# A four-stage attention and mixture-of-experts kernel: rounded first-expert weights made in the first attention's tail, second-expert biases loaded in the second's

## The chip, the cores and the metric

The kernel runs on one core of one Trainium2 chip. The metric is the device time of one execution in microseconds (us). Engines are named as in the profile: PE is the matmul engine (PEld its weight loads), DVE the vector engine, ACT the scalar engine, POOL the GpSimd engine and SP the sync engine, which here only issues DMA transfers. A name with q (SPq, ACTq) is that engine's instruction queue, where its DMA issues, drains and waits appear.

## What is computed

Two layers, each a gated cross-attention followed by a gated mixture of experts, all in float32. `x` is 32 batches of 100 tokens by 256, `ctx_768` is 32 batches of 361 rows by 192.

```python
x = x + tanh(g_xattn[0]) * L0_xattn(layernorm(x), ctx_768, Wq, Wk, Wv, Wo, bo)      # 8 heads of 64
x = x + tanh(g_ffn[0])   * L0_ffn(layernorm(x), router, w13, w2)                    # 8 experts, top 2, F = 512
x = x + tanh(g_xattn[1]) * L1_xattn(ctx_768, layernorm(x), mask, ...)               # 4 heads, keys of ctx and of x
x = x + tanh(g_ffn[1])   * L1_ffn(layernorm(x), Wg, W1, b1, W2, b2, W3, b3)         # 16 experts, top 4, F = 256

# L1_ffn, for each expert e, with a routing weight we per token:
h = silu(x2 @ W1[e].T + b1[e]) * (x2 @ W3[e].T + b3[e])
y = y + (h @ W2[e].T + b2[e]) * we[:, None]
```

## The kernel before

The program is a row of blocks, one after the other: a setup (L200), the first attention (`attention0`, L335), the first experts (`experts(…, 0)`, L1504), the second attention (`attention1`, L893) and the second experts (`experts1`, L1812). At the end of a block every engine runs a short drain of its own queue, and none starts the next block until the last engine has drained. In each block every engine has a program of its own, written out by hand as a list of steps; `at(i + k, step)` runs a step for batch `i + k` if there is such a batch, so that several batches are in flight, and semaphores hold the engines together. No planner decides the order: it is the order of the code, engine by engine.

`attention0` takes one batch of 100 tokens at a time. To keep float32 accuracy with faster matmuls, context and key/value weights are split in a rounded part (`c_hi`, `wk_hi`, `wv_hi`) and a rest (`c_lo`, `wk_lo`, `wv_lo`). SP loads `x` and `cT` (four transfers per batch, both double-buffered), stores the new `x` rows and the normalised rows, and, between the loads of batches 1 and 2, issues `fill` (L164 to L170: 16 issues of zeros or start values, for the tables, row buffers and outputs in memory that the later stages scatter into) and `load_attention1` (L180 to L190, the second attention's weights and scales). The load of `x` of batch b+2 waits for POOL's `xb` of batch b (L773), that of `cT` for the reads of `cT` of batch b. The routing steps at the end of each batch (L661 to L705 on DVE) choose two experts per token; POOL scatters table rows (L795) with the token's slot.

`experts(…, 0)` processes 57 tiles of 128 slots, sorted by expert. It starts with a *plan*: seventeen small DVE operations in a chain (L1555 to L1571) that turn the tokens per expert in `base` into each tile's expert, row and start, three PE transposes and three DVE casts (L1573 to L1575). SP's `slots` loads and POOL's gathers (L1512) wait for the plan. Its up-projection weights are split as well: ACT writes `w_hi` (rounded copy, 8 operations of 128x2048, L1679) and the rest is formed in place, `w13 - w_hi`: for experts 0 and 1 on POOL (L1531), for 2 to 7 on DVE after the plan (L1580). PE waits for all eight before its first tile. `w_hi` has a buffer of its own in this block.

`attention1` has a similar pipeline for the second layer. It begins on DVE with 16 memsets of `base`, a memset of the 25 padding rows of the whole `kv` buffer (L1323), of `ctx` padding, mask and a few others; the last one counts up `ready`, for which SP's first load, PE, ACT, POOL and DVE itself wait. In each round SP issues `x1in` of batch i+4, then `ctx` and mask of batch i+3. At its end the plan for the second experts is made here too, and SP and ACT write the end markers of each expert's rows (`empty_tails`, L890 and L891); SP ends its block after waiting for all of them.

`experts1` processes 115 tiles. SP loads rows (`xr`, L1885), ACT first issues three bias loads (L1906: `b1`, `b3`, `b2`, each broadcast to 128 partitions, 2048 KB) and then runs its tile work, DVE waits for all three and then adds `bias` to the up-projection `psG` into `pre` (L1843). `psG` holds two tiles, so PE can do tiles 0 and 1 before DVE has read `psG`.

## Time and profile before

| | us |
|---|---|
| median of 3 runs | 2112.01 (2111.58 to 2114.26) |
| the profiled execution | 2113.48 |
| its span in the trace | 2111.7 |
| engine busy in the span | PE 1932.3 (92%), DVE 1338.0, POOL 1147.6, ACT 930.0 |
| first attention, up to the release of its block | to 733.4 |
| first experts | 733.4 to 1071.2 |
| second attention | 1071.2 to 1727.5 |
| second experts | 1727.5 to the end |

The profiled execution is 1.47 us above the median and its span 1.78 us shorter than its time. In a row of the timeline the first number is the start in us from the span's start, the second how long the piece took, then come engine, line, operation, output and inputs with shapes, the number of instructions taken together (x16), and in brackets the idle time of the engine before it with what ended it. Where several instructions are taken together in one row, the duration is from the first's start to the last's end.

### The profile page before, as it was taken

How to read it: one execution, taken by the hardware profiler on the slowest of the kernel's cores; microseconds unless marked ns; L12 is line 12 of the kernel's file. 1: busy time of each engine (PE TensorE's matmuls, PEld its weight loads, DVE VectorE, ACT ScalarE, POOL GpSimd, SP SyncE). 2: the span in 40 equal slices, each digit the busy share in tenths (PEclk: the TensorE clock that was granted, in tenths of full speed). 3: DMA queues.
4: the chain of work that ended last, by engine and by line, in shares of the span. 5: the costliest groups of instructions: out<-in, count | busy, mean ns of one | idle time of the engine just before them, and what ended most of it. 6: DMA issues, size and time to landing. Idle time of an engine off the chain costs nothing. (4 is left out here: it accounts for less than half of the span.)

```text
span 2111.7 us, 39938 instructions
## 1 busy us (share of the span) xinstructions
PE 1932.3 (92%) x11418; PEld 1348.0 (64%) x11418; DVE 1338.0 (63%) x4050; ACT 930.0 (44%) x2321; POOL 1147.6 (54%) x1375
## 2 busy tenths in 40 slices
PE   5999999999999459999939999999999839999997
PEld 4777777777777348888825555555555525666664
DVE  3677777777777453222336888888888734566564
ACT  2444444434343233233216767666667503333332
POOL 1344444444444345445526888888888723454554
PEclk8999999999999679999979999999999758999999
DMA  6011111111107013333311111111112754555555
GB/s 170 27 31 37 32 35 36 31 39 28 40 27 260 9 26 53 54 52 51 52 32 34 51 51 52 56 56 53 54 54 69 253 167 98 89 92 88 94 89 75
DMA packets 140294, 142.24 MB, mean 67 GB/s; under 512 B 31626, under 2 KB 130674, under 8 KB 139832
## 3 DMA queue, kind: packets, MB, share of 16 engines
q1 hardware_dynamic: 94282, 86.60, 13.9%
q0 software_dynamic: 37888, 44.51, 13.3%
q10 hardware_dynamic: 7918, 8.57, 1.3%
q8 instruction: 105, 1.72, 0.4%
q14 instruction: 101, 0.83, 0.1%
HBM read 89.88 MB, written 51.94 MB: 67 GB/s over the span
## 5 line engine op out<-in xcount | busy, mean ns | idle before, releaser
L779 POOL TENSOR_SCALAR prob<-prob,rc 100x363 f32<-100x363 f32 x256 | 157.0, 623 | 354.6 <-DVE rc L634 354.6
L1826 POOL DMA_INDIRECT out<-y,xr x115 | 178.0, 1548 | 210.2 <-DVE y L1859 138.1
L1932 PE MATMUL psG<-expert_w,xgT 128*128 x460 | 222.0, 606 | 3.0 <-ACT xgT L1893 3.0
L980 PE MATMUL psJ<-wkv,cTn 96*121 96x512 f32 x384 | 177.7, 600 | 0.0
L1843 DVE TENSOR_TENSOR pre<-psG,bias 128x512 f32<-128x512 f32 x115 | 79.5, 691 | 144.6 <-PE psG L1932 104.1
L558 ACT ACTIVATE prob<-psS,nm 100x361 f32<-100x361 f32 x256 | 141.5, 561 | 53.8 <-DVE nm L629 47.6
L1525 POOL DMA_INDIRECT acc<-y,slots x57 | 90.3, 1584 | 136.5 <-DVE y L1619 131.6
L629 DVE TENSOR_REDUCE nm<-psS 100x2 f32<-100x722 f32 x128 | 115.0, 898 | 70.8 <-PE psS L457 70.6
L1432 POOL DMA_INDIRECT rows<-row,pos_of x128 | 137.1, 1071 | 35.6 <-issue 30.1
L1596 DVE TENSOR_TENSOR hid<-psU,gate 128x512 f32<-128x512 f32 x57 | 39.4, 691 | 159.3 <-PE psU L1716 159.3
L1893 ACT ACTIVATE xgT<-psX 128x256 f32<-128x256 f32 x115 | 44.0, 383 | 212.6 <-PE psX L1923 131.9
L1411 POOL TENSOR_TENSOR rk<-rk,neghalf 121x12 f32<-121x12 f32 x64 | 126.8, 1982 | 5.3
L638 DVE COPY pT<-psT 121x600 f32<-121x600 f32 x128 | 99.1, 774 | 44.9 <-PE psT L465 44.7
L563 ACT ACTIVATE oT<-psO 128x100 f32<-128x100 f32 x128 | 32.3, 253 | 210.1 <-PE psO L478 206.7
L1949 PE MATMUL psD<-expert_w,hT 128*128 x460 | 119.7, 383 | 1.2 <-ACT hT L1903 1.2
L1107 ACT ACTIVATE kv<-psJ 121x512 f32<-121x512 f32 (+2 forms) x160 | 88.0, 550 | 69.6 <-PE psJ L980 68.9
L1932 PEld LDWEIGHTS psG<-expert_w,xgT 128*128 128x128 f32 x460 | 79.9, 194 | 60.5 <-issue 60.5
L465 PEld LDWEIGHTS psT<-ident,prob 100*121 100x121 f32 x768 | 95.0, 187 | 27.8 <-POOL prob L779 20.4
L544 ACT ACTIVATE kT<-psJ 128x361 f32<-128x361 f32 x128 | 60.9, 476 | 116.4 <-PE psJ L420 116.4
L457 PE MATMUL psS<-kT,qT 64*100 64x361 f32 x512 | 110.9, 507 | 0.7 <-ACT prob L558 0.7
L465 PE MATMUL psT<-ident,prob 100*121 100x100 f32 x768 | 108.8, 278 | 2.4 <-POOL prob L779 2.4
L1754 PE MATMUL psD<-expert_w,hT 128*128 x456 | 108.0, 380 | 1.6 <-ACT hT L1674 1.6
(307 smaller groups left out, 5110.1 us busy)
## 6 DMA issues: line engine op xcount, KB each, us to landing
xr<-rows SPq DMA_DIRECT2D x115, 136.5 KB
expert_w<-in_L_ffn_moe_w SPq DMA_DIRECT2D x8, 1024.0 KB
bias<-in_L_ffn_b ACTq DMA_DIRECT2D x3, 2048.0 KB, 15.9
ctx<-in_ctx SPq DMA_DIRECT2D x32, 181.5 KB
cT<-in_ctxT SPq DMA_DIRECT2D x32, 180.5 KB
cT<-in_ctxT SPq DMA_DIRECT2D x64, 90.2 KB
expert_w<-in_L_ffn_moe_w SPq DMA_DIRECT2D x8, 512.0 KB
expert_w<-in_L_ffn_W1T SPq DMA_DIRECT2D x16, 256.0 KB
```

What stands on the lines that cost most here:

```text
L457: t.matmul(psS[0:N, h, 0:S], qT[rows, b % 2, p, :], kT[rows, b % 2, p, :], start=True, stop=True).then_inc(s_mm, 1)
L465: mm = t.transpose(psT[0:CH, h, j * N:(j + 1) * N], prob[:, (2 * p + h) % 4, j * CH:(j + 1) * CH], ident[0:N, 0:N])
L558: s.activation(prob[:, q, 0:S], psS[0:N, h, 0:S], ACT.Exp, bias=nm[:, q:q + 1], accum_out=rs[:, q:q + 1]).then_inc(exp_done, 1)
L629: v.tensor_reduce(nm[:, q2:q2 + 2], psS[0:N, :, 0:S], AX, ALU.max, negate=True).then_inc(max_done, 1)
L779: g.tensor_scalar(prob[:, q, :], prob[:, q, :], rc[:, q:q + 1], 1.0, ALU.mult, ALU.mult).then_inc(prob_done, 1)
L980: mm = t.matmul(ph[0:rows, 0:cols], lhs, wt[:, k, :], start=k == 0, stop=k == 1)
L1411: g.tensor_tensor(rk[:, b % 3, lo:hi, :], rk[:, b % 3, lo:hi, :], neghalf[0:CH, 0:1].unsqueeze(2).to_broadcast([CH, hi - lo, H1]), ALU.pow ...
L1432: g.indirect_dma_start(rows, bass.IndirectOffsetOnAxis(pos[:, b % 4, k:k + 1], 0), row[:, b % 4, :], None).then_inc(slots_out[b % 2], 16)
L1754: mm = t.matmul(psD[:, r, 0:D], hT[:, r, k, :], w2[:, bass.ds(e, 1), k, :], start=k == 0, stop=k == KF - 1)
L1826: g.indirect_dma_start(acc, bass.IndirectOffsetOnAxis(row_token[:, j % RING, :], 0), y[:, j % 4, :], None, compute_op=ALU.add).then_inc(sc ...
L1932: mm = t.matmul(psG[:, r, :], xT[:, r, k, :], w13[:, bass.ds(e, 1), k, :], start=k == 0, stop=k == 1)
L1949: mm = t.matmul(psD[:, r, 0:D], hT[:, r, k, :], w2[:, bass.ds(e, 1), k, :], start=k == 0, stop=k == KF - 1)
```

## The change

Line numbers of code after the change are those of the changed file. The change does six things.

1. **Buffers.** `w_hi` (now `c["w13_hi"]`) gets fixed space that lies over a slab of 64 KB per partition; `attention0`'s big buffers (`wk`, `wv`, `cT`, `c_hi`, `c_lo`, `kT`, `vv`, `qT`, `prob`) are views of the same space. In the second attention `ctx`, `sq`, `kv` and `prob` are views of a second slab, `late`, and the experts' biases (`b2`, then `b1` and `b3`) are other views of it.
2. **Weights.** The eight ACT copies and the rests of experts 0 to 2 move to the last rounds of `attention0`: copies 0 and 1 after the last `oT`, copy 2 after the last `xmT`, copies 3 to 7 at the end; rest 0 on DVE after the last normalisation, rests 1 and 2 at the end of DVE's program. Rests 3 to 7 stay with the experts, on DVE. POOL makes none.
3. **Plan.** The first experts' plan moves to the end of `attention0`, ahead of rests 1 and 2, with its transposes in `psY`.
4. **Start of `attention0` on SP.** `x` and `cT` of batch 2 are loaded before `fill`; `load_attention1` is issued in round 2, after the context load of batch 5.
5. **Start and rounds of `attention1`.** The `kv` memset covers only the first two of the five column blocks of each buffer (25x3072 for 25x7680; which of the three buffers a batch uses is shifted by one) and moves to POOL, which counts up `padded`; ACT and POOL wait for that. `ready` is counted up by the `ctx` memset, and only SP and DVE wait for it, SP after the first `x1in`. Context loads are issued before the `x1in` load of the same round, the other memsets follow.
6. **Biases.** SP issues them as five transfers in the last rounds of `attention1`: `b2` after the store of batch 29, `b1` and `b3` of experts 0 to 5 after that of batch 30, the rest when PE has done the last `oT`. ACT's three issues in `experts1` go.

```diff
@@ attention0, SP
-                for b in range(2):
+                for b in range(3):
                     load_x(b)
                     if b == 0:
                         s.wait_ge(ready, 1)
                     load_c(b)
                 fill(s, dram, c)
-                load_attention1(nc, s, a, c)
-                load_x(2)
-                load_c(2)
...
                     if b + 3 < B:
                         load_c(b + 3)
+                    if b == 2:
+                        load_attention1(nc, s, a, c)
@@ attention0, ACT
+                    if i == B:
+                        s.wait_ge(c["experts0_loaded"], 16 * W0_LOADS)
+                        s.wait_ge(k_mm, 4 * B)
+                        s.wait_ge(v_mm, 3 * B)
+                        make_high(s, c, range(0, 2))
...
+                    if i == B:
+                        make_high(s, c, range(2, 3))
...
+                s.wait_ge(s_mm, H0 * B)
+                s.wait_ge(o_mm, pairs * B)
+                make_high(s, c, range(3, E0))
@@ attention0, DVE
                     at(i - 1, y_norm)
+                    if i == B:
+                        make_low(v, c, range(0, 1))
...
+                steps = Count(plan)
...
+                v.tensor_copy(c["tile_r"][:, :], psY[0:1, P:2 * P])
+                make_low(v, c, range(1, 3))
@@ attention1, SP
-                s.wait_ge(ready, 1)
                 for i in range(-4, B + 1):
+                    if i == -3:
+                        s.wait_ge(ready, 1)
+                    at(i + 3, load_c)
                     at(i + 4, load_x)
-                    at(i + 3, load_c)
+                    if i == B - 1:
+                        s.wait_ge(ct_mm, 2 * B)
+                        s.wait_ge(ssB, B)
+                        s.wait_ge(o_mm, pairs * (B - 2))
+                        s.dma_start(b2, a["L1_ffn_b2"].partition_broadcast(P)).then_inc(c["bias_in"], 16)
+                    if i == B:
+                        s.wait_ge(o_mm, pairs * B)
+                        load_bias(s, 6, E1)
                     at(i - 1, store)
+                    if i == B - 1:
+                        s.wait_ge(o_mm, pairs * (B - 1))
+                        load_bias(s, 0, 6)
@@ attention1, DVE
-                for e in range(E1):
-                    v.memset(c["base"][:, e:e + 1], float(e * REGION))
-                v.memset(kv[96:CH, :, :, :], 0.0)
-                v.memset(ctx[96:CH, :, NCH - 1, :], 0.0)
+                v.memset(ctx[96:CH, :, NCH - 1, :], 0.0).then_inc(ready, 1)
...
+                for e in range(E1):
+                    v.memset(c["base"][:, e:e + 1], float(e * REGION))
@@ attention1, POOL
-                g.wait_ge(ready, 1)
+                g.memset(kv[96:CH, :, 0:2, :], 0.0).then_inc(padded, 1)
+                g.wait_ge(padded, 1)
@@ experts, POOL
-                if L0:
-                    for e in range(2):
-                        g.wait_ge(w_high, e + 1)
-                        g.tensor_tensor(w13[:, e].bitcast(F32R), w13[:, e], w_hi[:, e].bitcast(F32), ALU.subtract).then_inc(w_low, 1)
-                g.wait_ge(plan, PLANNED + 1)
@@ experts, DVE (after the plan, which is gone from here)
                 if L0:
-                    for e in range(2, E):
...
+                    make_low(v, c, range(3, E))
@@ experts1
-                for k in range(3):
-                    s.dma_start(bias[:, :, k, :], a[("L1_ffn_b1", "L1_ffn_b3", "L1_ffn_b2")[k]].partition_broadcast(P)).then_inc(bias_in, 16)
...
-                v.wait_ge(bias_in, 16 * 3)
+                v.wait_ge(c["bias_in"], 16 * BIAS_LOADS)
```

In the order listings a row is one instruction or several alike (x2): line, operation, output, inputs and the output's shape. On SP at the start of the first attention, from the load of batch 1 on, before and after (`cT_117` is `cT`; `table`, `xn`, `acc`, `out` and `rows` are filled from a buffer of zeros, `expert_w`):

```order
L354 DMA cT<-in_ctxT 64x361
L164 DMA table<-expert_w 128x512
L164 DMA table<-expert_w 6x512
L167 DMA xn<-expert_w 128x256
...
L189 DMA wr<-in_L_ffn_WgT 128x2x16
L190 DMA bo<-in_L_xattn_bo 100x256
L345 DMA x<-in_x 100x256
L352 DMA cT<-in_ctxT 128x361
```

```order
L396 DMA cT_117<-in_ctxT 64x361
L387 DMA x<-in_x 100x256
L394 DMA cT_117<-in_ctxT 128x361
L395 DMA cT_117<-in_ctxT 64x361
L396 DMA cT_117<-in_ctxT 64x361
L175 DMA table<-expert_w 128x512
```

The loads of batch 2 moved ahead of all 16 fill issues, and the weight loads of the second attention are no longer between.

On DVE at the end of the first attention (the branch is the end of the block's program, the next one the start of the experts'), from the last steps of the plan on, before and after:

```order
L1570 TENSOR_REDUCE tilet<-tilefirst 128x1
L1571 SCALAR_TENSOR_TENSOR tilet<-tilet,landed 128x1
L1573 CAST tile_s<-psX 1x128
L1574 CAST tile_e<-psX 1x128
L1575 CAST tile_r<-psX 1x128
L1580 TENSOR_TENSOR expert_w<-expert_w,w_hi 128x2048 x6
L1586 TENSOR_TENSOR xg_lo<-psX,xg_hi 128x256
```

```order
L839 SCALAR_TENSOR_TENSOR tilet<-tilet,landed 128x1
L841 CAST tile_s<-psY 1x128
L842 CAST tile_e<-psY 1x128
L843 CAST tile_r<-psY 1x128
L317 TENSOR_TENSOR expert_w<-expert_w,w_hi 128x2048 x2
L377 UNCONDITIONAL_BRANCH
L1640 UNCONDITIONAL_BRANCH
L317 TENSOR_TENSOR expert_w<-expert_w,w_hi 128x2048 x5
L1649 TENSOR_TENSOR xg_lo<-psX,xg_hi 128x256
```

The plan and two of the rests now stand before the block's end, and the experts' block starts on DVE with five rests where it had the plan and six.

On SP at the end of the second attention, after the change (before, four `out` stores stand there in a row, and then the same `base_i` row):

```order
L1014 DMA out<-x 100x256 x2
L1025 DMA late<-in_L_ffn_b 128x4096
L1014 DMA out<-x 100x256
L979 DMA late<-in_L_ffn_b 128x6x256
L980 DMA late<-in_L_ffn_b 128x6x256
L979 DMA late<-in_L_ffn_b 128x10x256
L980 DMA late<-in_L_ffn_b 128x10x256
L1014 DMA out<-x 100x256
L984 TENSOR_LOAD base_i
```

Five bias transfers stand between and around the last stores, ahead of SP's part of `empty_tails`.

## Rows read from the trace of the kernel before

**Rows 1.** The page, part 2: the span in 40 slices of 52.8 us, PE's lines.

```profile
PE   5999999999999459999939999999999839999997
...
PEclk8999999999999679999979999999999758999999
```

**Rows 2.** Windows: length, busy of PE to POOL, granted clock, DMA share, GB/s.

```profile
40.00:50.00 10.00, 8.44 (x40) 7.00 (x42) 4.46 (x9) 2.48 (x7) 2.52 (x5) 0.50 0.01 2
...
50.00:60.00 10.00, 10.00 (x59) 7.25 (x56) 4.14 (x9) 3.26 (x11) 1.39 (x4) 0.82 0.18 47
```

**Rows 3.** Timeline, start of the first attention: POOL, SP queue, ACT, PE.

```profile
23.81 0.72 POOL L773 TENSOR_TENSOR xb<-x,bo 100x256 f32<-100x256 f32 x1
...
34.49 1.30 SPq L354 DMA_DIRECT2D cT<-in_ctxT  x1
...
40.09 0.81 ACT L550 ACTIVATE c_hi<-cT 128x728 fp32r<-128x728 f32 x1 [6.03 <-DMA cT<-in_ctxT]
...
41.27 3.71 PE L430 MATMUL psJ<-xT,wq 128*128 128x100 f32 x16 [5.49 <-ACT xT L540]
```

**Rows 4.** Timeline, end of the first attention and start of the first experts.

```profile
719.24 0.17 DVE L661 COPY sc<-psY 100x8 f32<-100x8 f32 x1 [1.95 <-PE psY L499]
...
723.18 0.21 DVE L687 TENSOR_SCALAR slot<-slot,tmp 100x1 f32<-100x1 f32 x1
...
733.47 14.51 ACT L1679 ACTIVATE w_hi<-expert_w 128x2048 fp32r<-128x2048 f32 x8 [12.53 <-PEq L335]
...
735.61 4.39 DVE L1565 TENSOR_TENSOR tilet<-tile,tilet 128x1 f32<-128x1 f32 x1
...
740.22 4.25 DVE L1567 SCALAR_TENSOR_TENSOR tilet<-tilet 128x1 f32<-128x1 f32 x1
...
747.56 13.30 DVE L1580 TENSOR_TENSOR expert_w<-expert_w,w_hi 128x2048 fp32r<-128x2048 f32 x6
...
751.12 1.81 POOL L1512 DMA_INDIRECT xg<-xn,slots  x1 [6.67 <-DMA slots<-table]
...
761.11 0.66 PE L1708 MATMUL psX<-ident,xg 128*128 128x128 f32 x2 [14.37 <-DVE expert_w L1580]
```

**Rows 5.** POOL's drain at the end of the first attention: duration ns, start us.

```profile
L335 POOLq DRAIN  x1: 5297/5297/5297, 727.9 to 727.9; - x1
```

**Rows 6.** Timeline, start of the second attention.

```profile
1073.75 6.46 DVE L1323 MEMSET kv<- 25x7680 f32 x1 [1.93 <-issue]
...
1083.22 0.43 DVE L1198 BATCH_NORM_STATS2 st<-x1in 100x6 f32<-100x256 f32 x1 [2.15 <-DMA x1in<-acc]
...
1084.27 0.32 SPq L914 DMA_DIRECT2D m<-in_mask  x1
...
1087.35 0.88 DVE L1182 BATCH_NORM_STATS2 cst<-ctx 121x6 f32<-121x192 f32 x3 [3.49 <-DMA m<-in_mask]
```

**Rows 7.** Timeline, end of the second attention and start of the second experts.

```profile
1702.09 0.29 SPq L920 DMA_DIRECT2D out<-x  x1
...
1713.70 11.19 SPq L891 DMA_DIRECT2D rows<-rows  x8
...
1727.62 9.54 ACTq L1906 DMA_DIRECT2D bias<-in_L_ffn_b  x3
...
1728.68 10.30 SPq L1885 DMA_DIRECT2D xr<-rows  x8
...
1737.74 3.78 PE L1932 MATMUL psG<-expert_w,xgT 128*128 x4 [2.47 <-ACT xgT L1893]
...
1749.51 0.69 DVE L1843 TENSOR_TENSOR pre<-psG,bias 128x512 f32<-128x512 f32 x1 [30.48 <-DMA bias<-in_L_ffn_b]
...
1757.28 1.88 PE L1932 MATMUL psG<-expert_w,xgT 128*128 x4
```

**Rows 8.** Timeline, one round in the middle of the second attention.

```profile
1429.59 0.31 SPq L914 DMA_DIRECT2D m<-in_mask  x1
...
1434.38 0.42 DVE L1198 BATCH_NORM_STATS2 st<-x1in 100x6 f32<-100x256 f32 x1
```

More of the change, by code:

```diff
@@ L281, in router_tiles, with bias_views, make_high, make_low @@
     )
+def bias_views(c):
+    b2 = c["late"][:, 0:E1 * F1].rearrange("p (e f) -> p e f", e=E1)
+    b13 = c["late"][:, E1 * F1:3 * E1 * F1].rearrange("p (e k f) -> p e k f", e=E1, k=2)
+    return b2, b13
+BIAS_LOADS = 5
+def make_high(s, c, which):
+    w13, w2 = expert_views(c, 0)
+    w_hi = c["w13_hi"]
+    for e in which:
+        s.activation(w_hi[:, e], w13[:, e], ACT.Copy).then_inc(c["w13_high"], 1)
+def make_low(v, c, which):
+    w13, w2 = expert_views(c, 0)
+    w_hi = c["w13_hi"]
+    for e in which:
+        v.wait_ge(c["w13_high"], e + 1)
+        v.tensor_tensor(w13[:, e].bitcast(F32R), w13[:, e], w_hi[:, e].bitcast(F32), ALU.subtract).then_inc(c["w13_low"], 1)
 def attention0(nc, maker, a, dram, c):
@@ L534, in _ @@
                     at(i, values, 2)
+                t.wait_ge(plan, PLANNED - 1)
+                t.matmul(psY[0:1, 2 * P:3 * P], tf[:, 5:6], ident[:, :], start=True, stop=True)
+                t.matmul(psY[0:1, 0:P], tf[:, 2:3], ident[:, :], start=True, stop=True)
+                t.matmul(psY[0:1, P:2 * P], tf[:, 3:4], ident[:, :], start=True, stop=True).then_inc(plan, 1)
             @block.scalar
@@ L1057, in y_logits @@
                     mm.then_inc(lg_mm, 1)
-                t.wait_ge(ready, 1)
                 for i in range(-3, B + 2):
@@ L1635, in _ @@
             def _(s):
-                s.wait_ge(plan, PLANNED + 1)
                 def load(j):
@@ L1676, in _ @@
                 if L0:
-                    s.wait_ge(w_loaded, w_total)
-                    for e in range(E):
-                        s.activation(w_hi[:, e], w13[:, e], ACT.Copy).then_inc(w_high, 1)
+                    pass
                 else:
@@ L1800, in experts1 @@
         xT = sb("xgT1", [P, 2, 2, P])
-        bias, pre = sb("bias1", [P, E, 3, F]), sb("pre1", [P, 2, 2 * F])
+        pre = sb("pre1", [P, 2, 2 * F])
+        b2, b13 = bias_views(c)
         gate, hid, hT = sb("gate1", [P, 2, F]), sb("hid1", [P, 2, F]), sb("hT1", [P, 2, KF, P])
```

159 lines of the change are left out of this document (83 added, 76 removed).

## The prediction

> **What bounds the kernel now.** I read the page's busy slices first. PE is at nine tenths or more in both attentions and the second experts and nearly that in the first experts; it dips at four places: the first slice and the three changes of block [rows 1]. The granted clock dips at the same places: PE comes back from idle time at a lower clock. So inside the stages only less PE work would help, and this change removes none; what it can win lies in the four dips. The windows and the timeline say what each waits for.
>
> Start of the first attention: SP issues the context of batch 2 only at about 34.5, behind the fill and the second attention's weights; ACT waits 6.03 us for it and PE then has an idle 5.49 [rows 3]. After it PE runs at 0.50 of its clock in 40 to 50 and at 0.82 in 50 to 60 [rows 2]. Start of the first experts: the block is released at 733.4 because POOL's drain ends last [rows 5]; DVE then works through the plan until 747.56, two of its steps taking 4.39 and 4.25 us, then through six rests, 13.30 us, and PE begins at 761.11, released by DVE [rows 4]. Start of the second attention: DVE is free only at 1083.22 - 2.15 = 1081.07, after a 6.46 us memset, and SP's first load waits for that; context statistics begin at 1087.35 [rows 6]. Start of the second experts: ACT's queue is held 9.54 us by bias issues, DVE waits 30.48 us for the biases until 1749.51, and PE starts the up-projection of its fourth tile at 1757.28 [rows 7].
>
> **A, order on SP at the start.** In the new order x of batch 2 waits for POOL's `xb` of batch 0, which ends at 23.81 + 0.72 = 24.5, and its context is issued right behind, at about 25 to 26, against 34.5. ACT wanted it at 40.09 - 6.03 = 34.06 [rows 3], so it has 8 us to arrive. The wait of 5.49 goes. The lower clock behind it goes too: from 41.27 to 60 PE did 8.73 x 0.50 + 10 x 0.82 = 12.6 us of work at full clock in 18.7 us [rows 2], 6.2 lost. I take off 1 us for short waits that were hidden behind the long one. A = 5.49 + 6.2 - 1.0 = 10.7; bounds 5.5 (the wait only) and 11.7. The fill now starts some 3 us later and the weight loads two rounds later: nobody needs the latter before 1071, and SP's issues in round 2 hold up loads that are a whole round early.
>
> **B, end of the first attention and start of the first experts.** One ACT copy is 14.51 / 8 = 1.81 us, one rest on DVE 13.30 / 6 = 2.22 [rows 4]. Rest 0 goes in after the last normalisation, where DVE was idle for 1.95 until 719.24: from 717.29 to 719.51, so what follows is 0.27 late, and DVE's attention work ends at 723.18 + 0.21 + 0.27 = 723.66. The plan took from 733.5 to 747.56, 14.1 us; two steps stalled for 4.39 and 4.25 where a step of that size takes 0.21, as at 723.18 [rows 4]. I put the stalls down to POOL's two rests, which run then and now go. So the plan takes 14.1 - 8.2 = 5.9: until 729.5, where DVE had been idle. Rests 1 and 2 follow until 734.0. ACT is no limit: even if its eight copies began only at 723.2, copy 2 would be there at 728.6 and copy 7 at 737.7. POOL's drain would end at 727.9 + 5.3 + 0.3 = 733.5 [rows 5], DVE at 734.0 with a short drain behind it, so the release moves from 733.4 to about 734.4. Then five rests, 11.1 us, to 745.5, and PE starts 0.25 later, as it did before, at 745.8. B = 761.11 - 745.8 = 15.3. What is late next is the gather of tokens: it needs SP's slots, which are loaded at once now. Before, the first gather came at 751.12, 3.6 us after the plan's end, and took 1.81 with DVE in its rests [rows 4]; the same from 734.4 has it at 738, well ahead. Bounds: 15.5, and 11.7 where the rests on DVE hold POOL's drain (below).
>
> On that the rows show: two small DVE steps grow to 4.39 and 4.25 us while POOL runs tensor operations of its own [rows 4], so the two engines do exclude each other, in that direction. The Trainium skill, "SBUF — State Buffer", section "SBUF: two separate sides", calls this an exclusive lock on a port pair shared by DVE and GpSimd, and adds that a transfer issued by GpSimd cannot write its descriptors while a DVE operation holds it. By that rule the rests would hold what POOL does in its tail and the gathers; the gather of 1.81 us under the rests shows that they don't stop it for long here.
>
> **D, start of the second attention.** The first context load now waits only for the release at 1071.2 and one short memset: `ready` at about 1071.8. The mask's issue, the last of the context's three, follows some 0.8 later (before, it came 3.2 after `ready`, behind two `x1in` loads as well; one issue takes 0.3 [rows 6, 8]), at 1072.6, and the statistics 1087.35 - 1084.27 = 3.08 behind that: 1075.7. D = 1087.35 - 1075.7 = 11.65. The `kv` memset is on POOL: 0.4 of the elements, 2.6 us at DVE's rate, while ACT and POOL first have work to do about 3 us after `ready`; at a third of DVE's rate it would take 7.8 us and cost some 2.5. `base` is needed only by the first routing, several rounds on. D between 9 and 12.
>
> **C, biases.** Six megabytes took from 1727.62 to 1749.51: 6.29 MB in 21.9 us, 287 GB/s [rows 7]. The last 2.5 MB are issued after PE's last `oT`, before the last store, which SP issued at 1702.09; 8.7 us of transfer, so landed by about 1711, ahead of the end markers at 1713.70. DVE's wait goes, and ACT's 9.54 us. Next in line is `xr` of tile 0: issued at 1728.68, there 2.15 later, if it takes what `x1in` took [rows 6], at 1730.8; transpose 0.66 [rows 4] and ACT copy, 1.3 in all, as PE's tile begins: 1732.1 instead of 1737.74. Up-projection of tile 0 at half clock 3.78, of tile 1 the same with 1 us between, to 1740.8; tile 2 to start at 1741. Tile 3 comes 3.0 later at full clock, or 5.6 if the clock is still low, as it was before from 1751.65 to 1757.28. From PE's start at 41.27 the clock was low until about 53.6 (0.82 as the mean of 50 to 60 [rows 2] is 3.6 us at half and the rest at full), 12 us; the same from 1731 is 1743, in the middle of this. I take 1744.5. C = 1757.28 - 1744.5 = 12.8; bounds 9 and 14.
>
> **In the rounds of the second attention** `x1in` is issued behind the context and mask instead of ahead. The mask goes out at 1429.59, so `x1in` at about 1430.0; DVE reads it at 1434.38 [rows 8]. 4.4 us stand against a landing of 2.15, so it costs nothing; it is the one edit that repeats, 29 times. The views over slabs change no instruction.
>
> **Sum.** 10.7 + 15.3 + 11.65 + 12.8 = 50.4. The profiled execution took 2113.48, so 2063.1; it lay 1.47 above the median, which leaves 2061.6, rounded to 2062.
>
> **Rivals.**
> 1. *The rests on DVE hold POOL's drain.* For it: the stalls above, and that rests 1 and 2 lie wholly beside the drain. Against it: the drain took 5.3 us before while DVE stood idle [rows 4, 5], so it waits for something else. Price up to 4.4 us: release at 738, PE at 749.4, B = 11.7, time 2065. Chance 0.14.
> 2. *Only the wait of A goes.* Other short gaps in the first rounds keep the clock low as long as before. For it: even in 40 to 50 PE was busy for only 8.44 of 10 us [rows 2]. Against: the clock rose after that in spite of it. A = 5.5, time 2067. Chance 0.10.
> 3. *The biases delay the tail of the second attention.* Up to 4 MB in the last 25 us run beside POOL's row scatters, which the block's end waits for. The Trainium skill, "DMA: Bandwidth & Descriptors", section "Issuing engines are not separate DMA queues", says that all transfers share 16 engines and interleave, whoever issues them; no row here shows the two together. If the last of them hangs over 1713.70, C falls to 4 to 9, time 2066 to 2070. Chance 0.07.
> 4. *`x1in` comes late.* Behind a batch's context it lands after 1434.4, and each of 29 rounds grows. At 5 us after its issue the loss is 0.6 a round, 17 us, time 2079: 0.03. *Slower than before* is the same mechanism from 6.1 us on: 50.4 / 29 = 1.7 us a round eats all that is won, at 7 us the time is 2137. Against it: nothing in the profile lands so late with the queues this empty. Chance 0.03.
> 5. *The change does nothing*, since each dip has a second cause as long as the first (the scatters' landing for the release, say): 2112. Chance 0.01.
>
> The forecast has 0.62, from 2055 to 2067 with its own bounds. The range 2053 to 2074 takes in rivals 1 to 3 and the terms' bounds together; above it stands 0.07. About 0.2% (4 us) is what a measurement of this kernel tells from no change. Faster by more 0.96, within it 0.01, slower 0.03.
>
> **What would show it.** PE without a gap near 36 and at full clock in 40 to 60; no operation near 4 us in the plan; five rests after a release at 734 and PE's first tile at 746; context statistics at 1075.7 minus A and B; DVE's first `pre` right behind the first tile; the second attention as long per round as before. I am wrong if a round there is longer, if the releases come later than the sum has them, or if POOL's drain stretches.

## The result, and the profile after

The changed kernel takes 2076.9 us in the median of 4 runs (2071.66 to 2087.18), against 2111.8 of before beside it (4 runs, 2109.17 to 2114.26): a ratio of 0.9841, interval 0.9801 to 0.9881. It is faster, but by 35 us, not by 50; 2062 was forecast, with 2053 to 2074 as the range, and the time lies above it. Its profiled execution took 2076.01 us, its span 2074.3. The spread of the runs is wider as well: 15.5 us over four runs, where before had 5. It goes with PE's granted clock: the mean over the span was 0.966 in the fastest run and 0.957 in the slowest.

The block releases (the row of DVE's event at the end of each block) cut both spans in stages. The sums of the prediction are put against them; a release that comes later by the plan and two rests is counted in the first stage, and PE's earlier start in the second.

| stage | before | after | won | forecast |
|---|---|---|---|---|
| first attention, to its release | 733.4 | 725.3 | 8.1 | 9.7 |
| first experts | 337.8 | 322.1 | 15.7 | 16.3 |
| second attention | 656.3 | 655.9 | 0.4 | 11.65 |
| second experts | 384.2 | 371.0 | 13.2 | 12.8 |

Three stages gave what was forecast, within 1.6 us. The second attention gave next to nothing: 0.4 us.

The page, part 2, lines of PE, as [rows 1]: the first slice is fuller and its clock is at nine tenths or more; the three dips at the block changes are still there, each shallower in at least one of the two lines (the first two in PE's, the last in the clock's).

```profile
PE   6999999999999579999959999999999839999997
...
PEclk9999999999999689999979999999999859999999
```

**Start.** The timeline of SP's queue and ACT, as [rows 3]: the first context load of batch 2 goes out at 24.86 instead of behind 33, and ACT's rounding of it has no wait in brackets any more.

```profile
24.86 0.35 SPq L394 DMA_DIRECT2D cT<-in_ctxT  x1
...
34.35 0.82 ACT L595 ACTIVATE c_hi<-cT 128x728 fp32r<-128x728 f32 x1
```

The windows that answer to [rows 2] (length, busy time of PE, PEld, DVE, ACT, POOL, granted clock, DMA share, GB/s): PE is at its full clock and busy for 19.66 of 20 us.

```profile
40.00:50.00 10.00, 9.66 (x66) 7.04 (x67) 5.60 (x11) 3.26 (x11) 3.55 (x8) 1.00 0.17 48
...
50.00:60.00 10.00, 10.00 (x83) 7.99 (x83) 5.75 (x11) 4.91 (x15) 3.32 (x6) 1.00 0.01 2
```

The copy of the router's scores (the row that stands at 719.24 in [rows 4], one in each batch) comes 9.97 us earlier in batch 0 and 10.05 in batch 29, but only 8.45 in the last. In between lies the tail: PE idles 2.12 us there in both kernels, and the granted clock, 1.00 before it and 0.66 after it in the trace of before, fell earlier in the trace of after, 0.78 and then 0.54 (windows of 5 us each: 690 to 700 before, 680 to 690 after). Worked out from these, the time at half clock there was 3.4 us before and 6.8 after, which costs PE up to 1.7 us more of its work.

**End of the first attention, start of the first experts.** The timeline of ACT, POOL, DVE and PE, as [rows 4]:

```profile
702.20 3.70 ACT L309 ACTIVATE w_hi<-expert_w 128x2048 fp32r<-128x2048 f32 x2
...
708.49 3.29 POOL L880 DMA_INDIRECT table<-slot,pos  x1 [0.27 <-issue]
...
708.59 2.29 DVE L317 TENSOR_TENSOR expert_w<-expert_w,w_hi 128x2048 fp32r<-128x2048 f32 x1
...
710.79 0.16 DVE L716 COPY sc<-psY 100x8 f32<-100x8 f32 x1
...
714.97 0.15 DVE L823 TENSOR_TENSOR tilef<-base,region 128x8 f32<-128x8 f32 x1
...
720.62 4.47 DVE L317 TENSOR_TENSOR expert_w<-expert_w,w_hi 128x2048 fp32r<-128x2048 f32 x2
...
725.41 11.10 DVE L317 TENSOR_TENSOR expert_w<-expert_w,w_hi 128x2048 fp32r<-128x2048 f32 x5 [0.33 <-PEq L377]
...
728.38 2.40 POOL L1610 DMA_INDIRECT xg<-xn,slots  x1 [10.20 <-DMA slots<-table]
...
736.61 0.66 PE L1767 MATMUL psX<-ident,xg 128*128 128x128 f32 x2 [16.71 <-DVE expert_w L317]
```

Rest 0 sits in the gap (2.29 us from 708.59), rests 1 and 2 take 4.47, five more 11.10 from the release on. The plan (L823, the first of its 17 steps, at 714.97) runs until 720.62: 5.65 us, no step above 0.28. The first gather is issued at 728.38, well before PE begins at 736.61. Beside the rests POOL's transfers take longer to issue: the table scatter at 708.49 takes 3.29 us, the next one, without a rest beside it, 0.99.

POOL's drain, as [rows 5], and the release:

```profile
L377 POOLq DRAIN  x1: 5297/5297/5297, 719.8 to 719.8; - x1
...
L377 DVEq DRAIN  x1: 4959/4959/4959, 720.2 to 720.2; - x1
...
L377 DVEq EVENT_SEMAPHORE  x1: 21/21/21, 725.3 to 725.3; - x1
```

The drain is as long as before to the nanosecond, though rests 1 and 2 lay beside it from 720.62 to 725.1. DVE's drain, 0.25 us before, now lasts 4.96, as long as its rests, and ends with POOL's.

**Start of the second attention**, timeline as [rows 6]: the mask is issued 1.4 us behind the release of 1047.4, POOL's memset takes 2.65 us, and the statistics begin 4.95 us behind the release, where it was 16.15. So term D is there, 11.2 us of it.

```profile
1047.45 2.65 POOL L1539 MEMSET late<- 25x3072 f32 x1 [4.96 <-POOLq L1602]
...
1048.77 0.32 SPq L1008 DMA_DIRECT2D m<-in_mask  x1
...
1052.35 0.88 DVE L1287 BATCH_NORM_STATS2 cst<-late 121x6 f32<-121x192 f32 x3 [2.17 <-DMA m<-in_mask]
```

**Second experts**, timeline as [rows 7]: the end markers go out as long as before, PE's first tile begins 4.4 us after the release of 1703.3, `pre` waits for PE and no longer for a transfer, and tile 3 starts at 1720.30, 17.0 after the release. Before it was 29.8: 12.8 us.

```profile
1689.87 10.84 SPq L985 DMA_DIRECT2D rows<-rows  x8
...
1707.66 3.78 PE L1985 MATMUL psG<-expert_w,xgT 128*128 x4 [0.56 <-ACT xgT L1948]
...
1711.67 0.69 DVE L1898 TENSOR_TENSOR pre<-psG,late 128x512 f32<-128x512 f32 x1 [16.48 <-PE psG L1985]
...
1720.30 1.88 PE L1985 MATMUL psG<-expert_w,xgT 128*128 x4
```

**The rounds of the second attention.** From the statistics of the first batch to those of the last it takes 546.03 us before (1087.35 to 1633.38) and 558.13 after (1052.35 to 1610.48). Here are the missing 12 us. A round of the middle, as [rows 8], SP's queue and DVE: the context's first load, the mask's, behind it now `x1in`, and the statistics that wait for the mask to land.

```profile
1402.13 0.31 SPq L1006 DMA_DIRECT2D late<-in_ctx  x1
...
1402.89 0.32 SPq L1008 DMA_DIRECT2D m<-in_mask  x1
...
1403.32 0.28 SPq L997 DMA_DIRECT2D x1in<-acc  x1
...
1406.08 0.88 DVE L1287 BATCH_NORM_STATS2 cst<-late 121x6 f32<-121x192 f32 x3 [1.30 <-DMA m<-in_mask]
```

From the mask's issue to the statistics it is 3.19 us here, 3.02 in the round of before shown in [rows 8] (mask at 1429.59), of which these are the first context load and the statistics:

```profile
1428.82 0.31 SPq L912 DMA_DIRECT2D ctx<-in_ctx  x1
...
1432.61 0.88 DVE L1182 BATCH_NORM_STATS2 cst<-ctx 121x6 f32<-121x192 f32 x3 [1.13 <-DMA m<-in_mask]
```

Over the rounds from the eighth on the mean from the mask's issue to the statistics is 2.89 us before and 3.27 after, DVE waits 0.99 us a round before and 1.40 after, and the mean round is 18.21 and 18.61 us. These 24 rounds make 9.6 of the 12.1 us; the other 2.5 are in the first seven, which are irregular in both traces. The waits over 450 us in the middle of the stage (engine, tile and line that waited, releaser: us in total, times, longest), before and after:

```profile
DVE cst L1182 <- DMA m<-in_mask: 23.6, 25, 1.5
...
POOL crs L1385 <- DVE cmv L1186: 11.2, 25, 0.9
```

```profile
DVE cst L1287 <- DMA m<-in_mask: 32.1, 24, 2.0
...
POOL crs L1489 <- DVE cmv L1291: 19.3, 24, 1.7
```

DVE waits longer for the landing, and POOL in its turn longer for DVE.

### The profile page after: what moved, and what is told of

Same layout as the page of the kernel before. It is cut to its first block and busy times, and to the rows that moved or that the text cites. A ratio compares the mean times of both kernels' runs of the same rounds, so it can differ in the third digit from the quotient of the medians.

```text
span 2074.3 us, 39938 instructions
## 1 busy us (share of the span) xinstructions
PE 1929.3 (93%) x11418; PEld 1345.2 (65%) x11418; DVE 1329.4 (64%) x4051; ACT 930.3 (45%) x2321; POOL 1144.8 (55%) x1374
## 5 line engine op out<-in xcount | busy, mean ns | idle before, releaser
L1898 DVE TENSOR_TENSOR pre<-psG,late 128x512 f32<-128x512 f32 x115 | 79.6, 692 | 128.7 <-PE psG L1985 112.5
L1212 ACT ACTIVATE late<-psJ 121x512 f32<-121x512 f32 (+2 forms) x160 | 88.0, 550 | 70.7 <-PE psJ L1086 70.7
```

## The experiments

Seven kernels look for what lengthened the rounds, five take the terms of the sum one by one. Theory 1: each round is a loop through the landing of context and mask, so whatever delays the landing lengthens all rounds. Theory 2: the slab's views or something else in the stage costs the time. Theory 3: `x1in` itself comes late, the prediction's rival. All results are medians; the kernel before ran beside each of three sets, at 2111.72 us (the first four kernels), 2114.20 (three buffers for mask and for context, start, biases) and 2111.52 (the other four). The kernel with x first ran in the first set alone, so a difference to it from another set carries 2 to 3 us of uncertainty beside the spread of the runs.

### The order in the rounds, undone and done alone

```diff
                 for i in range(-4, B + 1):
-                    at(i + 3, load_c)
+                    if i < -2:
+                        at(i + 3, load_c)
                     at(i + 4, load_x)
+                    if i >= -2:
+                        at(i + 3, load_c)
```

> The changed kernel with one thing undone: in the rounds of the second attention SP issues x1in before the context again (the start, with the first context ahead, stays). Theory 1 (the rounds are a loop in which DVE's statistics wait for the last of context and mask to land, and an x1in issued 0.4 us behind the mask delays that landing): mask issue to statistics falls from a mean of 3.25 us back to 2.9, 31 rounds get 0.35 to 0.4 us shorter, 2065 to 2067 us, and the runs lie closer together than the 2071.7 to 2087.2 of the changed kernel. Theory 2 (the longer rounds come from the buffers as views over one slab, or from anything else in the second attention): no change, 2077.

Measured: 2066.58 us (2063.16 to 2068.24, 5 runs), ratio 0.9783 (0.9767 to 0.9799). The kernel before with the opposite edit:

```diff
                 for i in range(-4, B + 1):
+                    if i >= -2:
+                        at(i + 3, load_c)
                     at(i + 4, load_x)
-                    at(i + 3, load_c)
+                    if i < -2:
+                        at(i + 3, load_c)
```

> The kernel before with one thing done: in the rounds of the second attention SP issues context and mask before x1in; nothing else of the change. Theory 1: 30 rounds longer by 0.35 to 0.4 us, 2122 to 2124 us, with a wider spread of runs. Theory 2: as before, 2112.

Measured: 2120.67 us (2119.37 to 2129.53), ratio 1.0040 (1.0027 to 1.0054). One swap of two lines is worth 10 us down in one kernel and 9 up in the other, so the views don't make these 10 us. The time from the first statistics to the last is 550.9 us here, 7.2 less than in the changed kernel's trace. The spread of the runs is 5 us here for 15.5 in the changed kernel, but other kernels with x first and two mask buffers have 2.5 to 15, so the spread proves nothing about the order.

### x1in held back until the context has landed

```diff
                     at(i + 3, load_c)
+                    if i >= -2 and i + 4 < B:
+                        s.wait_ge(c_in, 48 * (i + 4))
                     at(i + 4, load_x)
```

> The changed kernel, order as it is (context first), but x1in is issued only when the context and mask of the round have landed, so that it never travels beside them. Theory 1: mask issue to statistics back to 2.9 us; x1in then lands some 5 us after the mask's issue, where DVE reads it, so 2065 to 2070. Theory 3 (the rounds are longer because x1in itself comes late for DVE, as the prediction's rival had it): it is now 3 us later still, and the rounds grow by up to 3 us, to 2120 and more. Theory 2: 2077.

Measured: 2070.92 us (2068.95 to 2071.53), ratio 0.9806 (0.9790 to 0.9822), with x1in some 3 us later than in the changed kernel. DVE's wait falls to 1.14 a round, and it is still for the mask. Theory 3 falls: a later `x1in` makes the rounds shorter. What costs is that it travels beside the other two. (A store of `x` goes out behind the mask in every one of these kernels, 0.41 us behind it in the kernel before. Here nothing follows the mask for 3.4 us and the statistics come 2.98 us behind it, as against 2.89 with the store, so the store costs nothing that shows; the load does.)

### The mask issued ahead of the context

```diff
-                def load_c(b):
+                def load_mask(b):
                     if b >= 2:
-                        s.wait_ge(ct_mm, 2 * (b - 1))
                         s.wait_ge(mask_done, b - 1)
                     if b >= 1:
                         s.wait_ge(c_in, 48 * b)
+                    s.dma_start(m8[:, b % 2, :], a["mask"][b].partition_broadcast(N)).then_inc(c_in, 16)
+
+                def load_c(b):
+                    if b >= 2:
+                        s.wait_ge(ct_mm, 2 * (b - 1))
...
                     at(i + 4, load_x)
                     if i >= -2:
+                        at(i + 3, load_mask)
                         at(i + 3, load_c)
```

> As the first kernel of this set (x1in first), and the mask's load, which needs no context buffer, is issued right behind x1in, half a round before the context. Theory 1: the last of the two context loads is now issued 0.41 us earlier than the mask was and nothing travels behind it: the wait falls by 0.4 to 0.9 us a round, 2040 to 2055 us, until PE (busy 97 to 98% there) holds the rounds. Theory 2: as the first kernel of this set.

Measured: 2109.80 us (2103.38 to 2118.08, 10 runs), 43 us more than the first kernel: nearly all of the 45 that the first kernel had won. I had expected a gain. The rows of one round, POOL, SP's queue and DVE:

```profile
1415.81 1.00 POOL L1515 TENSOR_SCALAR mb<-m 100x361 f32<-100x361 uint8 x1
...
1416.84 0.29 SPq L1004 DMA_DIRECT2D m<-in_mask  x1
...
1417.57 0.35 SPq L1011 DMA_DIRECT2D late<-in_ctx  x1
...
1422.06 0.88 DVE L1295 BATCH_NORM_STATS2 cst<-late 121x6 f32<-121x192 f32 x3 [2.28 <-DMA late<-in_ctx]
```

The mask did not go out early at all. SP held it until POOL's mask operation of two batches before had ended (1415.81 + 1.00), since that frees its buffer, and the context went out behind it. And in this order the landing takes longer: 4.9 us from the first context load (1417.18) to the statistics, where it is 3.79 in the round of [rows 8] (1428.82 to 1432.61) and 3.95 in the one shown of the changed kernel (1402.13 to 1406.08), both with the mask last. As a mean of the rounds from the eighth on it is 4.57 us, and 3.76 in the first kernel. The mask is one row of 361 bytes copied to 100 partitions. The rounds are 19.8 us on average, 1.5 more than in the first kernel: 0.3 because the mask is issued ahead of the context, 0.8 by the landing. The rest isn't the loads themselves: most rounds are 19.2 to 19.5 us, but three are 22.4 and one is 20.7, and in each of these the granted clock fell to half while PE was busy throughout, as here, in a round of 22.4:

```profile
1382.00:1392.00 10.00, 10.00 (x16) 4.18 (x15) 5.95 (x28) 3.40 (x7) 8.29 (x9) 0.50 0.16 45
```

So two things were learned: the order among the three loads costs a round 1.1 us, more than the place of `x1in`, and what SP waits for is the mask's buffer, not the context's. In the first kernel of the set the same is to be seen, POOL and then SP's first context load:

```profile
1452.52 1.01 POOL L1510 TENSOR_SCALAR mb<-m 100x361 f32<-100x361 uint8 x1
...
1453.59 0.31 SPq L1006 DMA_DIRECT2D late<-in_ctx  x1
```

POOL's operation ends at 1453.53 and the context goes out at 1453.59.

### Which buffer closes the loop

Three buffers for the mask, on top of the last kernel:

```diff
-        m8 = sb("m8", [N, 2, S], U8)
+        m8 = sb("m8", [N, 3, S], U8)
...
                 def load_mask(b):
-                    if b >= 2:
-                        s.wait_ge(mask_done, b - 1)
+                    if b >= 3:
+                        s.wait_ge(mask_done, b - 2)
...
```

> x1in first, as in the first kernel of the last set, and the mask in three buffers instead of two, its load issued right behind x1in, half a round before the context. In the traces SP issues the context within 0.1 us of the end of POOL's mask operation, whose buffer the next mask needs; the transposes that free the context's own buffer end 3 us earlier. Theory 1a (what closes the loop of a round is the mask's buffer): the context now goes out 3 us earlier and the mask isn't in its way; DVE's wait of 1.1 us goes, the round falls from 18.3 to what PE needs, 17.6 to 17.9, and the time to 2040 to 2052. Theory 1b (the context's own buffer or the landing itself closes it): 2060 to 2067.

Measured: 2049.58 us (2048.63 to 2051.09, 5 runs), ratio 0.9696 (0.9677 to 0.9716), the fastest kernel of the study: 27 us below the changed kernel's 2076.9 and 62 below the 2111.8 of before. The rows of one round, SP's queue and DVE:

```profile
1428.24 0.28 SPq L997 DMA_DIRECT2D x1in<-acc  x1
...
1428.61 0.30 SPq L1004 DMA_DIRECT2D m<-in_mask  x1
...
1428.97 0.33 SPq L1010 DMA_DIRECT2D late<-in_ctx  x1
...
1442.32 0.88 DVE L1295 BATCH_NORM_STATS2 cst<-late 121x6 f32<-121x192 f32 x3
```

All three loads go out together in the middle of a round, 13 us ahead of the statistics and not 3 as I had put it (the transposes that free the context's buffer were done a round earlier than I had read: 21 us ahead of the context's load in the trace of the first kernel). DVE doesn't wait, from the eighth on the rounds are 17.7 us (the mean 17.72), and the spread of the runs is 2.5 us. And three buffers for the context instead, the mask with two:

```diff
-        for parts, dims in ((CH, (2, NCH, C)), (CH, (NCH + 2, I1)), (CH, (3, NCH + 2, 2 * I1)), (N, (4, K1))):
+        for parts, dims in ((CH, (3, NCH, C)), (CH, (NCH + 2, I1)), (CH, (3, NCH + 2, 2 * I1)), (CH, (2, 2, nch, N))):
...
-        ctx, sq, kv, prob = views
+        ctx, sq, kv, pT = views
+        prob = sb("prob1", [N, 4, K1])
...
                 def load_c(b):
+                    if b >= 3:
+                        s.wait_ge(ct_mm, 2 * (b - 2))
                     if b >= 2:
-                        s.wait_ge(ct_mm, 2 * (b - 1))
                         s.wait_ge(mask_done, b - 1)
...
```

> x1in first, the mask in two buffers as ever, and the context in three (to make room, the exponentials get a buffer of their own, pT goes over the slab and a scratch tile of the plan over qT). Theory 1a: SP still waits for POOL's mask operation before it issues the context, so nothing is won: 2065 to 2068. Theory 1b: the context goes out a round earlier, the wait goes, 2040 to 2052.

Measured: 2068.69 us (2063.65 to 2071.73), ratio 0.9778 (0.9751 to 0.9805): no gain over the first kernel. POOL's mask operation and SP's context load stand as they stood:

```profile
1456.77 1.00 POOL L1512 TENSOR_SCALAR mb<-m 100x361 f32<-100x361 uint8 x1
...
1457.84 0.31 SPq L1008 DMA_DIRECT2D late<-in_ctx  x1
```

So the loop is: the mask's operation on POOL, SP's loads, their landing, DVE's statistics, POOL's scale factors that wait for these, and by POOL's order its mask operation again. That the third mask buffer opens the loop is shown by the time. The part through POOL is read from the traces: in both the kernel before and the changed one SP issues the first context load 0.06 to 0.09 us behind the end of the mask's operation in every round from the third on, and a round from the eighth on splits in

| | before | after |
|---|---|---|
| end of the mask's operation to the first context load | 0.06 | 0.06 |
| that load to DVE's statistics (the landing) | 3.66 | 4.06 |
| statistics to the end of POOL's mask operation of the batch before | 14.49 | 14.49 |
| round | 18.21 | 18.61 |

The whole growth is in the landing, and in the shown round of the first kernel POOL works from the scale factors (1440.34) to the end of the mask's operation (1453.53) without a gap over 0.3 us. The context's own buffer has no part in it.

### The changed kernel with nothing but a third mask buffer

```diff
-        m8 = sb("m8", [N, 2, S], U8)
+        m8 = sb("m8", [N, 3, S], U8)
...
                     if b >= 2:
                         s.wait_ge(ct_mm, 2 * (b - 1))
-                        s.wait_ge(mask_done, b - 1)
+                    if b >= 3:
+                        s.wait_ge(mask_done, b - 2)
...
```

> The changed kernel as it is, context ahead of x1in, with one edit: the mask has three buffers, so that SP needs POOL's mask operation of the batch before only. Context, mask and x1in still travel together. If the order cost its 10 us only because the landing lay in the loop that the mask's buffer closed, the context now goes out some 3 us before it is needed, the later landing is hidden, the rounds are 17.7 us as with the mask issued early, and the time is 2048 to 2053. If three transfers together cost something of their own: 2060 or more.

Measured: 2052.74 us (2050.70 to 2053.09, 5 runs), ratio 0.9717 (0.9704 to 0.9730), with rounds of 17.72 us. The order of the change costs the rounds nothing once the landing is out of the loop. The 3.2 us to the fastest kernel lie elsewhere in the traces: the second attention takes 632.2 us here and 632.8 there. One point of the expectation didn't come about: `x1in` no longer travels with the other two, because the context now goes out much earlier.

```profile
1409.04 0.39 SPq L1009 DMA_DIRECT2D m<-in_mask  x1
...
1413.37 0.28 SPq L997 DMA_DIRECT2D x1in<-acc  x1
```

That three transfers together cost nothing then is shown by the kernel with the mask issued early and in three buffers, where they stand 0.4 us apart.

### The terms of the sum, one by one

Four of the five are made on the kernel with x first (2066.58), the third on the kernel before. SP's order at the start as before the change:

```diff
-                for b in range(3):
+                for b in range(2):
...
                 fill(s, dram, c)
+                load_attention1(nc, s, a, c)
+                load_x(2)
+                load_c(2)
...
-                    if b == 2:
-                        load_attention1(nc, s, a, c)
```

> x1in first, and SP's order at the start of the first attention as before the change: fill and the second attention's weights ahead of x and context of batch 2. The prediction's term A, measured as 9.97 us from batch 0 to 29 and 8.45 at the last batch of the trace after the change: this should be 8.5 to 10 us slower than the first kernel, 2075 to 2077. If the gain at the start is lost in the tail of the stage anyway: 2067 to 2072.

Measured: 2077.30 us (2073.35 to 2082.66), 10.7 more in the medians. That A is there is shown; its size is not shown as closely as the two equal numbers look, since the runs spread over 9 us and the set differs. In this execution the granted clock behind the gap was 0.74 in 40 to 50 and 1.00 in 50 to 60, better than in [rows 2], and the first attention was released at 732.7, 7.5 later than the 725.2 of the kernel with x first.

Rests 1 and 2 after the release:

```diff
-                make_low(v, c, range(1, 3))
...
-                    make_low(v, c, range(3, E))
+                    make_low(v, c, range(1, E))
```

> x1in first, and the rests of experts 1 and 2 on DVE after the release instead of before it: seven of 2.22 us there. Before, DVE's and POOL's drains at the end of the first attention both ended within 0.2 us (725.1). The prediction's term B (POOL's drain is not held by the rests): the release stays where it is and PE begins 4.4 us later, 2070 to 2072. Its first rival (the rests hold POOL's drain): the release comes up to 4.4 us earlier and eats this, 2066 to 2068.

Measured: 2068.07 us (2067.45 to 2078.78, 5 runs), 1.5 more, and with runs of 2067.5 to 2078.8 that settles nothing. The trace, of the slowest of these runs, does, DVE and PE first, then POOL's drain:

```profile
723.30 15.50 DVE L317 TENSOR_TENSOR expert_w<-expert_w,w_hi 128x2048 fp32r<-128x2048 f32 x7 [4.47 <-PEq L377]
...
738.90 0.66 PE L1769 MATMUL psX<-ident,xg 128*128 128x128 f32 x2 [20.85 <-DVE expert_w L317]
```

```profile
L377 POOLq DRAIN  x1: 5297/5297/5297, 717.7 to 717.7; - x1
```

Seven rests take 15.50 us, and PE begins 25.9 us after the last step of DVE's routing (712.99), where it is 21.8 in the kernel with x first (714.71 to 736.49): 4.1 of the 4.4. POOL's drain begins 4.7 us after that last step in both and is 5297 ns with the rests beside it and without. The prediction's first rival falls.

The kernel before with its two POOL rests on DVE:

```diff
-                if L0:
-                    for e in range(2):
-                        g.wait_ge(w_high, e + 1)
-                        g.tensor_tensor(w13[:, e].bitcast(F32R), w13[:, e], w_hi[:, e].bitcast(F32), ALU.subtract).then_inc(w_low, 1)
...
-                    for e in range(2, E):
+                    for e in range(E):
```

> The kernel before with one thing done: the rests of experts 0 and 1 on DVE too, after the plan, none on POOL. The prediction put the two stalled steps of the plan (4.39 and 4.25 us for 0.17) down to POOL's rests: the plan falls from 14.1 to 5.9 us, eight rests take 17.7 for 13.3, PE begins 3.8 us earlier, 2107 to 2109. If the stalls have another cause they stay: PE 4.4 us later, 2116 to 2117.

Measured: 2110.91 us (10 runs, 2104.42 to 2114.64 but for one of 3424.42), ratio 0.9991 (0.9978 to 1.0004): no difference that the time shows, and the 3 us that I expected are inside the spread. The trace shows the mechanism, DVE's two steps that took 4.39 and 4.25 us in [rows 4], and the rests:

```profile
735.52 0.16 DVE L1561 TENSOR_TENSOR tilet<-tile,tilet 128x1 f32<-128x1 f32 x1
...
735.90 0.16 DVE L1563 SCALAR_TENSOR_TENSOR tilet<-tilet 128x1 f32<-128x1 f32 x1
...
739.15 17.70 DVE L1576 TENSOR_TENSOR expert_w<-expert_w,w_hi 128x2048 fp32r<-128x2048 f32 x8
```

The steps are 0.16 us, the plan goes from 733.39 to 739.15, and the eight rests end at 756.85, 4.0 earlier than before. The stalls were POOL's rests: one of 4.53 us from 735.46, one of 4.52 from 739.93 (L1531). Both stalled steps read two inputs (L1565, L1567); the step between them, with one (L1566), took 0.15 us beside the second rest. The Trainium skill, "SBUF — State Buffer", section "SBUF: two separate sides", has the rule of the port pair shared by the two engines; this pair of traces agrees.

The three bias loads on ACT again:

```diff
-                        s.dma_start(b2, a["L1_ffn_b2"].partition_broadcast(P)).then_inc(c["bias_in"], 16)
...
-                        load_bias(s, 6, E1)
...
-                        load_bias(s, 0, 6)
...
+                s.dma_start(b13[:, :, 0, :], a["L1_ffn_b1"].partition_broadcast(P)).then_inc(c["bias_in"], 16)
+                s.dma_start(b13[:, :, 1, :], a["L1_ffn_b3"].partition_broadcast(P)).then_inc(c["bias_in"], 16)
+                s.dma_start(b2, a["L1_ffn_b2"].partition_broadcast(P)).then_inc(c["bias_in"], 16)
                 x_transposed(0)
```

> x1in first, and the three bias loads on ACT at the start of the second experts again, 2 MB each, into the same buffers. Term C: 12.8 us slower than the first kernel, 2079 to 2080. If loading them in the tail of the second attention costs that tail something that comes back here: less, 2072 to 2078.

Measured: 2077.94 us (2076.40 to 2078.92), 11.4 more, 12.8 expected. The wait is back as it was:

```profile
1715.82 0.69 DVE L1890 TENSOR_TENSOR pre<-psG,late 128x512 f32<-128x512 f32 x1 [30.99 <-DMA late<-in_L_ffn_b]
```

And the start of the second attention with all memsets on DVE ahead of `ready`:

```diff
-                    if i == -3:
+                    if i == -4:
                         s.wait_ge(ready, 1)
...
-                v.memset(ctx[96:CH, :, NCH - 1, :], 0.0).then_inc(ready, 1)
-                v.wait_ge(ready, 1)
...
+                v.memset(kv[96:CH, :, :, :], 0.0)
+                v.memset(ctx[96:CH, :, NCH - 1, :], 0.0)
...
+                v.tensor_scalar(c["token"][:, :], c["token"][:, :], float(-TOKENS), None, ALU.add).then_inc(ready, 1)
...
-                g.memset(kv[96:CH, :, 0:2, :], 0.0).then_inc(padded, 1)
-                g.wait_ge(padded, 1)
+                g.wait_ge(ready, 1)
```

> x1in first, and the start of the second attention as before the change: the memsets of base and of the whole kv on DVE ahead of ready, for which all engines wait. Term D, of which the trace after the change shows 11.1 us up to the first statistics: 2077 to 2078. If the first rounds gave that back anyway (they are irregular in both traces): 2067 to 2072.

Measured: 2074.58 us (2074.41 to 2082.78, 4 runs), 8.0 more, some 11 expected. The release is at 1045.6:

```profile
1048.19 6.46 DVE L1431 MEMSET late<- 25x7680 f32 x1 [1.64 <-issue]
...
1059.67 0.88 DVE L1290 BATCH_NORM_STATS2 cst<-late 121x6 f32<-121x192 f32 x3 [1.28 <-DMA m<-in_mask]
```

From the release to the statistics it is 14.1 us, 9.4 more than the 4.7 of the kernel with x first; the other 2 of the 11 came from the context going out ahead of the second `x1in`, which this kernel keeps (0.4 us behind the first `x1in` here, 2.4 in the kernel before). So D was real, and most of it stayed: 8.0 of 9.4.

## Why the prediction was wrong

**What bounds the kernel.** Right for the four dips. Wrong where it said that inside the stages only less PE work would help. In the second attention PE was busy 97 to 98%, and I took that for PE-bound; DVE's wait of 1 us in every round was the sign that something else closed the round. With the wait gone the same work takes 17.72 instead of 18.21 us a round, without any PE work less.

**A**, 10.7 forecast: 9.97 in the trace at batch 0, 10.05 at batch 29, 7.5 at the release and 10.7 in the medians by undoing it. The stage kept 8.1 against 9.7; of the 1.6 that went between batch 29 and the last copy (10.05 to 8.45) most is the clock that fell earlier in the tail: in the trace with the biases back on ACT, where the first stretch at half clock there is 3.4 us as before, only 0.25 goes (11.19 to 10.94). The mechanism was right and the size within its bounds; that the medians give exactly 10.7 is chance.

**B**, 15.3 forecast: PE's first tile is 24.5 earlier, of which 8.45 are A's, so 16.05. The plan was 5.65 against 5.9, and both drains ended together at 725.1, where the working had DVE 0.5 us behind POOL. Right, and the rival on POOL's drain is refuted.

**D**, 11.65 forecast: 11.2 up to the first statistics; by undoing the memsets, which are 9.4 of it, 8.0. Right as a term, a little high.

**C**, 12.8 forecast: 12.8 at tile 3 in the trace, 11.4 by undoing it. Right (the last biases are 2.62 MB and not 2.5, which moves their landing by 0.4 us and changes nothing), with both of its parts: the last biases had landed before `pre` and the tail was no longer than before (the last statistics to the release, 94.1 before and 92.8 after).

**The rounds of the second attention**, forecast at no cost: this step failed. No other is off by more than 1.6 us in the table of stages, and with `x1in` first again the kernel takes 2066.58, inside the range. The working asked whether `x1in` would still reach its reader and found 4.4 us of slack against a landing of 2.15. That was true: DVE never waits for it. It didn't ask whose landing `x1in` would delay. The mask's had no slack: DVE already waited for it in each round. The rounds took 12.1 us more in the trace, about 0.4 a round and more than D had won; the order is worth 10.3 of them in the medians (2076.9 to 2066.58) and 9 in the kernel before. The mechanism that the fourth rival named (a late `x1in`) was the wrong one, though its price and its multiplier (rounds x delay) were of the right kind: at 0.4 us a round it would have said 2074 instead of 2079. It had 0.03.

With the slab's views and x first, the mean round is 18.32 to 18.37 us in four traces, 18.59 in the one with three context buffers and 18.69 in the one with the rests after the release, and 18.21 and 18.25 in the two traces of the old order and buffers. The two long ones are explained in part: each has stretches at half clock in rounds of 20.7 us, one in the first (at 1297) and two in the second (at 1408 and 1466), where the four have none. This is one of them, from the trace with the rests after the release:

```profile
1408.00:1414.00 6.00, 6.00 (x12) 2.79 (x11) 4.95 (x22) 2.84 (x5) 5.15 (x7) 0.50 0.23 61
```

What stays open: the landing is also longer there (3.98 and 4.04 us for 3.76 to 3.80) with the same order of loads, so something else lengthens it too in some executions; and the 0.1 us a round between the old code and the four, 2 to 3 us over the stage, of which most is in the landing as well (3.66 and 3.69 against 3.76 to 3.80). The views, the shifted buffer index or chance may be its cause. With the third mask buffer neither can be seen.

## What to carry to other kernels

An engine that is 97% busy may still not be what closes the loop: look for a short wait that recurs in every round, and follow the buffer behind it back to who frees it. Rounds that jump by 2 or 3 us have to be held against the granted clock before they are put down to the edit. A transfer that is moved has to be priced twice, by its own reader's slack and by the slack of those that it now travels with; the second had none here. When a small operand shares its semaphore and its load step with a large one, its buffer count decides when the large one may start: one more buffer of 361 bytes per partition was worth 24 us.

## What was not expected of the hardware

- Three loads issued 0.4 us apart land in a time that depends on their order: with the 361-byte mask broadcast to 100 partitions behind the two loads of the context it took 3.66 us (the kernel before) to 4.06 us (the changed kernel) on average from the first context issue to DVE's start, with the mask first 4.57 us, counted from the first context issue too.
- POOL's drain at the end of the first attention was 5297 ns in every trace, with DVE in 128x2048 operations beside it or idle, while an indirect transfer's issue on POOL grew from 0.99 to 3.29 us beside one such operation.
